# Writing out the last turn of an expert loop and dropping the group behind the last

## What is computed

```python
scores = (jnp.tanh(xf @ gate_w.T) + 1.0) * 0.5
vals, idx = jax.lax.top_k(scores.T, k)          # k = 8192 / 8 = 1024 rows for each expert
y = _layernorm(xf[flat_idx].reshape(k, n, d), ln_gamma, ln_beta)
h = jax.nn.gelu(jnp.einsum('knd,nfd->knf', y, fc1s) + b1s, approximate=True)
o = jnp.einsum('knf,ndf->knd', h, fc2s) + b2s
out = xf.at[flat_idx].add((o * kept_w[:, :, None]).reshape(k * n, d))
```

## The kernel before

| tile | offset | tile | offset |
|---|---|---|---|
| w_h (mixer's input weights) | 48544 | w2h2, w2l2 | 151872, 153920 |
| xt_h, xt_l | 114080, 122272 | w2h0, w2l0 | 156160, 158208 |
| idx | 142880 | w1h1, w1h3 | 160256, 168448 |
| w1h0, w1h2 | 143680, 147776 | w2h3, w2l3 | 172544, 174592 |
| yt_h1 | 176640 | hid_h0 to hid_h3 | 209408 and every 2048 |
| b1 | 222656 | hid_l0, hid_l1 | 217600, 219648 |
| | | hid_l2, hid_l3 (behind b1) | 223616, 225664 |

## Time and profile before

### The profile page before, as it was taken

The page is one execution under the profiler, slowest core; times in us unless marked ns, Lnnn a source line. Parts: engine busy times, 40 slices in busy tenths (PEclk is TensorE's granted clock), DMA queues, the critical chain, the costliest instruction groups (busy, mean ns, idle before and its releaser), DMA issues.

```text
span 2823.4 us, 40464 instructions
## 1 busy us (share of the span) xinstructions
PE 2758.5 (98%) x12170; PEld 2196.6 (78%) x12170; DVE 1857.0 (66%) x3098; ACT 1369.4 (49%) x2317; POOL 686.2 (24%) x1009
## 2 busy tenths in 40 slices
PE   7899999999999999999999999999999999999997
PEld 3578888888887777777788888888888888888886
DVE  8768888888877887788754555455554555455554
ACT  4644555455555555564544444444444444444443
POOL 4422222222222112124321122112221122112221
PEclk9999999999999999999999999999999999999999
DMA  9633323222223333326233042231422313314221
GB/s 348 241 119 105 97 82 97 90 89 95 91 96 97 105 105 105 105 75 199 80 83 83 16 127 54 69 87 26 113 69 47 104 32 100 82 23 121 39 46 16
DMA packets 118953, 265.11 MB, mean 94 GB/s; under 512 B 23968, under 2 KB 24160, under 8 KB 114784
## 3 DMA queue, kind: packets, MB, share of 16 engines
q1 hardware_dynamic: 84512, 164.83, 17.2%
q0 software_dynamic: 34240, 97.85, 14.8%
HBM read 208.86 MB, written 53.77 MB: 93 GB/s over the span
## 4 chain that ended last, share of the span: by engine, by line
PE 88%; DVE 6%; ACT 2%; issue 2%; DMA 1%; POOL 0%; DVEq 0%; ACTq 0%; POOLq 0%
PE po L1867 8%; PE po L1869 8%; PE po L1868 8%; PE ring L1458 8%; PE ring L1460 8%; PE ring L1459 8%; PE pb L1867 4%; PE pb L1869 4%; PE pb L1868 4%; PE pc L1869 4%; PE pc L1868 4%; PE pc L1867 4%; PE po L1491 3%; PE po L1493 3%; PE po L1492 3%
## 5 line engine op out<-in xcount | busy, mean ns | idle before, releaser
L1458 PE MATMUL ring<-xt_h,w_h 128*128 128x512 f32 x1024 | 402.6, 393 | 2.8 <-DVE xt_l L483 2.6
L1867 PE MATMUL po<-w2h,hid_h 128*128 128x512 f32 x1024 | 402.3, 393 | 1.0 <-DVE hid_l L1828 1.0
L1869 PE MATMUL po<-w2h,hid_l 128*128 128x512 f32 x1024 | 402.0, 393 | 0.0
L1868 PE MATMUL po<-w2l,hid_h 128*128 128x512 f32 x1024 | 401.9, 392 | 0.0
L1460 PE MATMUL ring<-xt_h,w_l 128*128 128x512 f32 x1024 | 401.0, 392 | 0.0
L1459 PE MATMUL ring<-xt_l,w_h 128*128 128x512 f32 x1024 | 398.7, 389 | 0.0
L1260 DVE SCALAR_TENSOR_TENSOR u<-xin,cw,u 128x512 f32<-128x512 f32 x384 | 288.5, 751 | 60.6 <-issue 28.7
L1795 ACT ACTIVATE hid<-pb,b1c 128x512 f32<-128x512 f32 x128 | 88.2, 689 | 410.7 <-PE pb L1869 410.7
L1718 POOL DMA_INDIRECT out_dram<-res,idx_c x64 | 101.3, 1583 | 738.5 <-DVE res L1854 724.2
L1828 DVE TENSOR_TENSOR hid_l<-hid,hid_h 128x512 fp32r<-128x512 f32 x128 | 88.7, 693 | 280.2 <-ACT hid_h L1799 280.2
L1828 DVE TENSOR_TENSOR hid_l<-xn_tail,hid_h 128x512 fp32r<-128x512 f32 x128 | 88.6, 692 | 241.8 <-ACT hid_h L1799 241.8
(11 more groups left out here) (207 smaller groups left out, 5959.9 us busy)
## 6 DMA issues: line engine op xcount, KB each, us to landing
wo<-wo_halves POOLq DMA_DIRECT2D x120, 512.0 KB, 4.0
w1r<-fc_in SPq DMA_DIRECT2D x130, 256.0 KB, 2.7
w2r<-fc_in SPq DMA_DIRECT2D x130, 256.0 KB, 3.0
g_x<-x_in SPq DMA_DIRECT2D x16, 1024.0 KB, 9.0
x_tail<-x_in SPq DMA_DIRECT2D x64, 256.0 KB, 2.7
out_dram<-res SPq DMA_DIRECT2D x64, 256.0 KB, 2.1
xt_rows<-g_xnt SPq DMA_DIRECT2D x15, 1024.0 KB, 10.6
rows<-xt_rows SPq DMA_DIRECT2D x15, 1024.0 KB, 5.9
```

Source lines behind the costliest of these rows:

```text
L1458: pe.matmul(ring[r % 2][:, :], w_h[:, r, q], xt_h[:, k, :], start=(k == 0), stop=False)
L1867: pe.matmul(dst, ah, bh, start=start, stop=False)
L1868: pe.matmul(dst, ah, bl, start=False, stop=False)
L1869: return pe.matmul(dst, al, bh, start=False, stop=stop)
```

## The change

The last pair of groups is written out behind the loop on TensorE, VectorE, ScalarE and GpSimd (loops over E-1 experts, then `pair(E - 1, last=True)`), and its second group leaves out everything that served group 16: the gathers, statistics, normalisation, transposes, their halves, the weights of slices 16 and 17, SyncE's four loads. `idx` and `b1` lose their spare entries, and the two memsets and `c_pad` go. Its core:

```diff
-        self.idx = m.sb("idx", [P, (2 * E + 1) * J], U32)
+        self.idx = m.sb("idx", [P, 2 * E * J], U32)
...
-        pool.memset(ew.idx[:, 2 * E * J:(2 * E + 1) * J], 0).then_inc(c_set, 1)
-        pool.wait_ge(c_set, 7 + 1)
+        pool.wait_ge(c_set, 6 + 1)
...
-    b1 = m.sb("b1", [P, (E + 1) * FT])
+    b1 = m.sb("b1", [P, E * FT])
...
-        for i in range(2):
-            sp.wait_ge(c_wl, 2 * ((G - 1) * FT + i + 1) + 1)
-            ew.load(sp, 0, i)
...
-        pool.memset(b1[:, E * FT:(E + 1) * FT], 0.0).then_inc(c_pad, 1)
...
-        with pool.Fori(0, E) as e:
+        def pair(e, last=False):
             for i in range(2):
                 g = 2 * e + i
-                gather(g + 1, 1 - i)
-                ew.inverse_std(pool, g + 1, ends.half)
-                gather_gates(g + 1, 1 - i)
+                if not (last and i == 1):
+                    gather(g + 1, 1 - i)
+                    ew.inverse_std(pool, g + 1, ends.half)
+                    gather_gates(g + 1, 1 - i)
                 scatter(g, i)
+
+        with pool.Fori(0, E - 1) as e:
+            pair(e)
+        pair(E - 1, last=True)
...
-                    next_high(e, i, s)
-                    if s - 1 in T_AT:
+                    if not (end and s + 2 >= FT):
+                        next_high(e, i, s)
+                    if s - 1 in T_AT and not end:
                         t_high(g + 1, T_AT.index(s - 1), 1 - i)
...
-                    if 3 <= s < 3 + J:
+                    if 3 <= s < 3 + J and not end:
                         ew.statistics(dve, g + 1, s - 3)
-                    w_low(dve, n + 2, s + 2)
+                    if not (end and s + 2 >= FT):
+                        w_low(dve, n + 2, s + 2)
...
-        dve.wait_ge(c_pad, 1 + 1)
         pair(0, True)
-        with dve.Fori(1, E) as e:
+        with dve.Fori(1, E - 1) as e:
             pair(e)
+        pair(E - 1, last=True)
...
-                    if s - 1 in T_AT:
+                    if s - 1 in T_AT and not (last and i == 1):
                         trn(g + 1, T_AT.index(s - 1))
                 last_shares(g)
+
+        with pe.Fori(0, E - 1) as e:
+            pair(e)
+        pair(E - 1, last=True)
```

More of the change, by code:

```diff
@@ L853, in out @@
         sp.wait_ge(self.c_out, 16 + 1)
-        sp.dma_start(self.ew.idx[:, 0:2 * E * J].rearrange("p (e c) -> p e c", e=E),
+        sp.dma_start(self.ew.idx[:, :].rearrange("p (e c) -> p e c", e=E),
                      self.slots_d.rearrange("(e h) l -> e (h l)", e=E)
@@ L1086, in gpsimd @@
             w_low(c)
-        ls.constants(pool, c_set, 7)
+        ls.constants(pool, c_set, 6)
         with pool.Fori(1, BPS) as b:
@@ L1235, in scalar @@
             act.wait_ge(sums.c_xt_store[i], 16 * (NB // 4 - i // 3) + 1)
-        act.wait_ge(c_set, 7 + 1)
+        act.wait_ge(c_set, 6 + 1)
         turn(0, True)
@@ L1245, in vector @@
         dve.wait_ge(sums.c_small_in, 16 * 8 + 1)
-        dve.wait_ge(c_set, 7 + 1)
+        dve.wait_ge(c_set, 6 + 1)
         def t_low(n, k, last=False):
@@ L1338, in prefix @@
                 dve.wait_ge(c_cnt, ROUNDS * BISECT_BLOCKS + 1)
-                dve.wait_ge(c_set, 13 + 1)
+                dve.wait_ge(c_set, 12 + 1)
                 ls.masks(dve)
@@ L1657, in stage_experts @@
     c_bias = m.count("f_bias")
-    c_pad = m.count("f_pad")
     c_b1 = m.count("f_b1")
@@ L1765, in first_bias @@
         sp.wait_ge(sums.c_ho, all_out + 1)
-        sp.dma_start(b1[:, 0:E * FT], t["b1"]).then_inc(c_bias, 16)
+        sp.dma_start(b1[:, :], t["b1"]).then_inc(c_bias, 16)
     sums.first_high, sums.first_low, sums.first_bias = first_high, first_low, first_bias
@@ L1785, in scalar, with pair @@
         act.wait_ge(ends.c_po, (NB - 1) * J + 1 + 1)
-        with act.Fori(0, E) as e:
+        def pair(e, last=False):
             for i in range(2):
                 g = 2 * e + i
+                end = last and i == 1
                 for s in range(FT):
@@ L1799, in scalar @@
                     act.copy(hid_h[s % 4][:, :], hid[s % 2][:, :]).then_inc(c_hh, 1)
-                    next_high(e, i, s)
-                    if s - 1 in T_AT:
+                    if not (end and s + 2 >= FT):
+                        next_high(e, i, s)
+                    if s - 1 in T_AT and not end:
                         t_high(g + 1, T_AT.index(s - 1), 1 - i)
+        with act.Fori(0, E - 1) as e:
+            pair(e)
+        pair(E - 1, last=True)
     def vector(dve):
@@ L1820, in tail, with pair @@
                 ends.finish(dve, NB - 1, s - 2)
-        def pair(e, first=False):
+        def pair(e, first=False, last=False):
             for i in range(2):
                 g = 2 * e + i
+                end = last and i == 1
                 for s in range(FT):
@@ L1829, in pair @@
                                       ALU.subtract).then_inc(c_hl, 1)
-                    if 3 <= s < 3 + J:
+                    if 3 <= s < 3 + J and not end:
                         ew.statistics(dve, g + 1, s - 3)
-                    w_low(dve, n + 2, s + 2)
+                    if not (end and s + 2 >= FT):
+                        w_low(dve, n + 2, s + 2)
                     if first and i == 0:
                         tail(s)
-                    if 3 <= s < 3 + J:
+                    if 3 <= s < 3 + J and not end:
                         ew.normalise(dve, g + 1, s - 3)
-                    if s == J + 3:
+                    if s == J + 3 and not end:
                         keep(g + 1, 1 - i)
@@ L1913, in tensor, with pair @@
         pe.wait_ge(sums.c_tl, (NB + 1) * KD + 1)
-        with pe.Fori(0, E) as e:
+        def pair(e, last=False):
             for i in range(2):
```

## The result

The changed kernel takes 2822.21 us in the median (22 runs, 2819.37 to 2822.92), the kernel before 2825.45 us (22 runs, 2823.99 to 2827.37): 3.2 us less, ratio 0.9986 with a 95% interval of 0.998 to 0.9992. The interval leaves out 1, so with 22 runs of each kernel a gain is measured, but one of less than the 0.2% that the prediction took as the least that can be told. The forecast was 2824.2 us, in a range of 2819.0 to 2827.5, from 2.4 us gained. The profiled execution took 2819.37 us, the fastest of its 22, so spans of two single profiles (2823.4 and 2817.6) must not be set against each other.

The account below looks back on a forecast made before the run. TensorE's own instructions were taken to bound the expert stage. Transposes 1.75, first result 0.45 and jump 0.2 sum to 2.4 us less, from 2826.62 to 2824.2 us, range 2819.0 to 2827.5: no measurable difference.

Parts of the forecast that it names:

- TensorE alone bounds the stage: Expert stage, start to last matmul: only TensorE's own instructions count, so other engines' dropped work there is worth nothing.
- Transposes: TensorE, group 15: four sets of four transposes go, 0.44 us each, 1.75 us in all, bounds 1.4 and 1.8.
- First result at the end: VectorE, after the last matmuls: without an unused low half the first result starts 0.45 us earlier, and GpSimd's scatters follow.
- The jump: TensorE's expert-stage loop: six jumps back instead of seven, 0.2 us gained, bounds 0 and 0.4 us.
- Leaving the loop: Exit from the expert-stage loop into straight code: costs 0, with one stall of 1.8 us as upper bound.
- Memsets and waits: The index and bias memsets and the c_pad wait: worth 0, at most the memsets' own 0.1 and 0.2 us.
- Layout: Tiles behind idx move by 32 or 96 bytes: 0, with 2.6 us allowed either way over 256 blocks.
- half of the hidden tiles falling in step: Rival, xt_h with w1h0 and w1h2: 128 bytes suffices, 64 blocks save 5.1 us, time 2819.1 us; chance 0.10.
- starts on a boundary of 64 bytes count: Rival, whole expert stage: the 32-byte move makes 192 short blocks long, 13.4 us lost, time 2837.6 us; chance 0.04.
- The eaten gain: Rival: a 1.8 us stall at TensorE's loop exit, or first scatter not the pace; 2826.0 or 2824.7 us; chance 0.14.

Follow-up runs that it names:

- the control: The changed kernel with a 32-byte tile ahead of w_h, moving every mixer and expert-stage tile alike; expert-stage matmuls took 1447.91 us.

## Why the prediction was right

- **TensorE alone bounds the stage**: right for group 15 and wherever the change acts; no work of the other engines changed its stretch, with the transposes back or out. "From the start of the stage" was too much: the earlier trace rows began at 1480 us, and at 1364.57 TensorE waits 1.05 us for VectorE. The kernel after has the same wait, so no term of the sum hung on it.
- **Transposes**, 1.75 us with 1.8 as the upper bound: 1.82 to 1.88 us. Right, a little over the bound. I took a set's cost from its own rows, 0.44 us; it is 0.46 to 0.47, since a block that steps at 227 ns otherwise has several steps of 231 to 236 ns behind a set.
- **First result at the end**, 0.45 us: 0.4 by the halves put back, and the scatters are paced by the first, as forecast. I had taken the 0.45 us between matmul and result from the second bank; on the first it is 0.50. The steps between the scatters gave 0.1 us more that I had not seen.
- **The jump**, 0.2 us: nothing that shows (net 1448.4 us with one jump less, 1448.4 before). I had divided the stage's "issue" waits among the jumps; most jumps cost nothing, while 25 of the 73 in the twelve profiles cost 0.04 to 0.35 us, and 0.1 us more in the step behind, with no pattern that I see.
- **Leaving the loop**, 0: right, a step of 231 ns, and of 226 to 236 in the ten other kernels that have the exit.
- **Memsets and waits**, 0: nothing shows in TensorE's start of either stage (the wait ahead of the first matmul of the expert stage is 1.40 us before and 1.38 after); they were not tried alone.
- **Layout**, 0 with 2.6 us either way: 1.0 us gained. This is the term that was mis-sized. Short blocks stayed short and no class fell wholly into step, as the remainders had it. But I priced a block by whether its own pairs are in step and put everything else at nothing: classes that are out of step moved by up to 1.2 ns a matmul, and some whose pairs kept their distance moved too (hidden blocks of slots 1 and 3 in odd groups and share blocks of slot 1 rose by 0.7 to 0.9 ns).

The terms measured are 1.8 + 1.0 + 0.5 = 3.3 us; the medians differ by 3.2. The forecast gain was 2.4: the layout gave 1.0 that the sum did not have, and the jump did not give its 0.2. Had the layout's move gone the other way by as much, which the sum could not tell, the gain would have been near 1.3 us; that part is luck. Some of the distance between 2824.2 and 2822.21 us is not the kernel's at all: I started from the median of three runs, 2826.62 us, and the 22 runs have 2825.45. Of the rivals, half of the hidden tiles falling in step did not happen: with a remainder of 128 bytes the blocks stay at 232.9 and 231.8 ns, and reach 227.1 and 228.7 only with none. That starts on a boundary of 64 bytes count is refuted by the changed kernel itself, whose short blocks moved by 32 bytes and stayed short, and by the control. The eaten gain did not come.
## What to carry to other kernels

When one engine bounds a stage without a wait, price a removed instruction on it by the distance of its neighbours' starts some way behind it, and look only at the very end for work of the other engines. Work for a turn that does not exist costs what it takes from the bounding engine and from the tail, here 0.1%, however much else it does. Where matmuls load float32 weights beside streaming float32 data, as here, compare the steps of equal blocks on different tiles early: laying the tiles multiples of 256 bytes apart gave 1.0% of the whole time. And before a stretch of one engine is compared between two profiles, look for steps that differ from profile to profile; a part without them, here one group, comes out alike to 0.01 us, while the whole stage as it stands shows 0.4 us (1447.99 - 1447.62) for a layout that is worth 1.0.

## What was not expected

**The step depends on distance to the nanosecond.** Blocks in the same slot of the same group parity repeat their pattern of steps to 1 ns in nearly all of the stage, whatever the other engines do at that time. With everything in step, a matmul of 512 columns takes 226.7 ns; hidden blocks out of step, with remainders of 64, 96, 128, 160 or 192 bytes, take 231.8 to 234.0. What in the chip makes it so no run here tells.

**The clock in the mixer's first turn makes most of the spread between runs.** With the placement of the changed kernel, turn 0 took 79.6 us in its own profile and 82.5 with the transposes back, which are 1300 us away. TensorE waits 2.6 us ahead of that turn and 1.5 us near its end. The windows of the kernel after and then of the one with the transposes back (granted clock: the third number from the end):

```profile
118.00:130.00 12.00, 11.43 (x52) 9.22 (x53) 5.93 (x11) 6.35 (x11) 0.91 (x5) 1.00 0.25 30
...
190.00:200.00 10.00, 8.32 (x34) 6.33 (x35) 7.23 (x15) 3.71 (x6) 2.44 (x4) 1.00 0.60 193
```

```profile
118.00:130.00 12.00, 11.01 (x43) 8.70 (x44) 5.02 (x11) 4.39 (x7) 0.80 (x5) 0.86 0.15 31
...
190.00:200.00 10.00, 8.24 (x30) 6.11 (x29) 9.14 (x18) 3.71 (x6) 2.81 (x9) 0.83 0.52 168
```

In the slow stretches the steps are 0.43 us, those of the 1.2 GHz level, six to eight at each place, so a place costs about 7 x 0.2 = 1.4 us. The kernel before has them once, at 192.9 us, the kernel after not at all: that is the 1.5 us of turn 0 in the first table. Over the profiles of this study turn 0 took 79.6 to 82.7 us, nearly the 3.5 us by which runs of one kernel differ. The kernel before and the one that is only written out show it best: their spans are 2823.4 and 2822.1 us, their turns 0 take 81.1 and 79.7 us, and without turn 0 they agree to 0.1 us. It is not bound to turn 0: in the profile with slots 0 and 2 in step the clock fell at 866.9 us too, and that turn took 78.4 us where the changed kernel's takes 76.7. The waits are there in every execution; why the clock falls in one and not in the next stays open.
